# Values of the gated attention projected for two head pairs at once with tokens on partitions, sent to batch order through HBM, in a one-core early-fusion kernel

## The reference, cut to what matters

```python
# x (16,3,96,96), x_txt (16,32): 36 patch tokens + 32 text tokens = 68 per batch, 16 batches, 1088 tokens
h = concat(patch_embed(x), text_embed(x_txt))         # (16, 68, 256)
n = layernorm(h)
q, k, v = n @ W_q, n @ W_k, n @ W_v                   # 16 heads of 64
a = sigmoid(n @ W_gate + b_gate)                      # (16, 68, 16, 64)
# for each batch and head, over the 68 tokens:
#   S = a_t[:, None] * S + k_t[:, None] * v_t[None, :];   o_t = q_t @ S
h = h + out @ W_o
h = h + moe(layernorm(h))                             # 8 experts, top 2 of them, 256 -> 512 -> 256
```

## Time and profile before

| | |
|---|---|
| median of 3 runs | 406.86 us (405.18 to 407.86) |
| the profiled execution | 408.7 us; span of its trace 407.0 us |
| mean granted PE clock | 0.934 of full speed |
| busy: PE, PEld, DVE, ACT, POOL | 344.7, 299.4, 222.7, 132.4, 131.1 us |
| attention (first projection to last mix) | 38.1 to 221.2 us |
| steady pair step | 22.6 to 22.8 us |

### The profile page before, as it was taken

How to read it: one execution, slowest core, us unless ns; L and a number is a source line. 1 busy time by engine, 2 the same in 40 slices (tenths; PEclk the granted TensorE clock), 3 DMA queues, 4 the chain that set the end, 5 groups by cost and what they waited for, 6 DMA issues and landing times.

```text
span 407.0 us, 7752 instructions
## 1 busy us (share of the span) xinstructions
PE 344.7 (85%) x2739; PEld 299.4 (74%) x2740; DVE 222.7 (55%) x329; ACT 132.4 (33%) x279; POOL 131.1 (32%) x124
## 2 busy tenths in 40 slices
PE   4883997989989898989998999883499999999900
PEld 3663987888888888888987887573378888888800
DVE  0048799468484948577582145458235545544325
ACT  1143661444536253444344011431023223323300
POOL 5120043221312212222013699103506555554310
PEclk9997998999999999999999999966589999999965
DMA  7810011010010710000001930003102221122155
GB/s 208 289 52 2 0 53 52 4 52 2 2 53 0 317 45 0 0 0 0 1 1 26 439 159 0 0 2 110 52 26 68 66 77 65 70 70 66 41 165 202
DMA packets 10791, 28.85 MB, mean 71 GB/s; under 512 B 2000, under 2 KB 6608, under 8 KB 10128
## 3 DMA queue, kind: packets, MB, share of 16 engines
q1 hardware_dynamic: 8336, 21.99, 14.9%
q0 software_dynamic: 2432, 6.56, 5.6%
HBM read 23.17 MB, written 5.37 MB: 70 GB/s over the span
## 4 chain that ended last, share of the span: by engine, by line
PE 64%; DVE 9%; issue 9%; POOL 8%; DMA 7%; ACT 1%; SPq 1%; DVEq 0%; POOLq 0%; ACTq 0%
PE ps L716 10%; PE ps L381 8%; PE ps L503 7%; PE ps L382 7%; PE ps L383 7%; PE ps L518 5%; POOL w1lo L1415 5%; DVE U L1048 4%; PE ps L488 4%; PE ps L695 3%; PE ps L697 3%; PE ps L696 3%; PE ps L706 2%; POOL w1hi L1413 2%; DMA pt<-patches 2%
## 5 line engine op out<-in xcount | busy, mean ns | idle before, releaser
L381 PE MATMUL ps<-xnhi,wlo 128*128 128x272 f32 x256 | 77.4, 302 | 16.1 <-DVE kU L1054 9.0
L382 PE MATMUL ps<-xnlo,whi 128*128 128x272 f32 x256 | 75.5, 295 | 0.0
L383 PE MATMUL ps<-xnhi,whi 128*128 128x272 f32 x256 | 75.2, 294 | 0.0
L381 PEld LDWEIGHTS ps<-xnhi,wlo 128*128 128x128 f32 x256 | 49.9, 195 | 19.2 <-DVE kU L1054 10.4
L1062 DVE RECIPROCAL invU<-U 128x272 f32<-128x272 f32 x32 | 56.7, 1813 | 0.0
L943 ACT ACTIVATE hr<-ps,b 128x128 f32<-128x128 f32 x96 | 27.4, 367 | 81.3 <-PE ps L706 81.3
L1367 POOL TENSOR_TENSOR qA<-qraw,invU 128x544 f32<-128x544 f32 x16 | 22.3, 1392 | 95.3 <-DVE invU L1062 75.5
L382 PEld LDWEIGHTS ps<-xnlo,whi 128*128 128x128 f32 x256 | 49.8, 195 | 0.0
L383 PEld LDWEIGHTS ps<-xnhi,whi 128*128 128x128 f32 x256 | 49.7, 194 | 0.0
L1048 DVE TENSOR_TENSOR_SCAN U<-u_g,first 128x544 f32<-128x544 f32 x16 | 29.8, 1865 | 28.9 <-ACT u_g L827 28.9
L716 PE MATMUL ps<-w,hr 128*128 x192 | 45.2, 379 | 0.0
(11 more groups left out here) (166 smaller groups left out, 526.3 us busy)
## 6 DMA issues: line engine op xcount, KB each, us to landing
wraw<-w_attn SPq DMA_DIRECT2D x8, 512.5 KB, 3.4
w<-w SPq DMA_DIRECT2D x1, 4096.0 KB, 15.2
w<-w SPq DMA_DIRECT2D x1, 3072.0 KB, 10.6
yin<-yrows SPq DMA_DIRECT2D x4, 384.0 KB, 4.5
wo<-w_o SPq DMA_DIRECT2D x1, 1024.0 KB, 14.0
w<-w SPq DMA_DIRECT2D x1, 1024.0 KB, 5.9
b<-b SPq DMA_DIRECT2D x1, 1024.0 KB, 17.1
xrows<-xrow SPq DMA_DIRECT2D x2, 512.0 KB, 3.0
```

The costliest lines, as they stand in the source:

```text
L381: pe.matmul(dst, slo, mhi[n], start=(i == 0), stop=False)
L382: pe.matmul(dst, shi, mlo[n], start=False, stop=False)
L383: last = pe.matmul(dst, shi, mhi[n], start=False, stop=(i == len(pairs) - 1))
```

## The change

The values are no longer projected pair by pair. For two pairs at a time (`k`, 256 value columns) the roles are exchanged: 128 tokens of the activations are the stationary operand, 256 columns of the value weights move, and the result has tokens on partitions. Nine token tiles (the last of 64 tokens) make five chunks `j` per two pairs: four of 12 matmuls with 256 columns and one of six. ACT copies each chunk from bank 6 to one of two `vst` buffers, SP stores it to the HBM array `vrows` (256 KB a chunk, the last 64 KB), and `load_values(hp)` brings one pair back as 68 tokens on partitions, 16 batches of 128 columns: 557 KB in pieces of 512 bytes. So `vT`, the transposes (L488) and two ACT copies (L841, L847) go. The chunks are placed between the other work of earlier steps (`EVEN`, `ODD`, `FIRST`). Scores take the heads alternately. Queries, scores and mixes are interleaved; the last group of pair `hp-2` is mixed after the first gate of step `hp`; DVE takes scan, mask, scan, keys, keys. The gate's exponential goes straight to `u_g`. Steps 6 and 7 are written out without chunks. SP loads w1 one expert per step instead of six at once.

```diff
-MATS = 4
+MATS = 3
@@ sync
+            def store_values(k, j):
+                sp.wait_ge(s_vev, VC * k + j + 1)
...
+                    sp.dma_start(vrows[k, at:at + 2 * P].rearrange("(q p) d -> p q d", p=P), vst[j % 2][:]
+                                 ).then_inc(s_vst[j % 2], 16)
...
+            def load_values(hp):
+                for i in range(2):
+                    sp.wait_ge(s_vst[i], stored(hp // 2 + 1, i))
                 if hp >= 2:
+                    sp.wait_ge(s_omm, 4 * (hp - 1))
+                c = (hp % 2) * P
+                sp.dma_start(vb[hp % 2][0:T], vrows[hp // 2, :, c:c + P].rearrange("(b t) d -> t b d", t=T)
+                             ).then_inc(s_vb[hp % 2], 16)
...
+            load_value_weights(1)
+            for j in range(VC):
+                store_values(0, j)
+            load_values(0)
+            load_values(1)
+            for hp in range(1, HP):
+                if hp + 1 < HP:
+                    sp.wait_ge(s_wlo, hp)
+                    sp.dma_start(wraw[(hp + 1) % 2][:], w_attn[hp + 1, :, 0:WA + 1]).then_inc(s_wload[(hp + 1) % 2], 16)
+                k = hp // 2 + 1
+                if k < IT:
+                    for j in (range(VC) if hp == 1 else range(3) if hp % 2 == 0 else range(3, VC)):
+                        store_values(k, j)
+                if hp % 2 and k + 1 < IT:
+                    load_value_weights(k + 1)
+                if hp >= 2:
+                    load_values(hp)
+                if hp <= EARLY_W:
+                    sp.dma_start(w1[:, hp - 1], w_1[:, hp - 1]).then_inc(s_w1, 16)
@@ tensor, pair_step (before: projections, then turn_values / pair_scores / mix for each group)
+                project(hp, par, GATE, 0)
+                if not early(hp, 2):
+                    mix(hp - 2, par, G - 1, loaded[par])
+                pe.wait_ge(s_qraw, 2 * hp)
+                project(hp, par, GATE, 1)
...
+                pair_scores(hp - 1, 1 - par, 0)
+                pe.wait_ge(s_exp, 2 * hp + 1)
+                project(hp, par, KEY, 0)
+                chunk(1)
+                pe.wait_ge(s_exp, 2 * hp + 2)
+                project(hp, par, KEY, 1)
+                mix(hp - 1, 1 - par, 0, loaded[1 - par])
+                chunk(2)
+                pair_scores(hp - 1, 1 - par, 1)
+                pe.wait_ge(s_ku, 2 * hp + 1)
+                project(hp, par, QUERY, 0)
+                chunk(3)
+                mix(hp - 1, 1 - par, 1, loaded[1 - par])
+                pair_scores(hp - 1, 1 - par, 2)
+                chunk(4)
+                pe.wait_ge(s_ku, 2 * hp + 2)
+                project(hp, par, QUERY, 1)
+                mix(hp - 1, 1 - par, 2, loaded[1 - par])
+                pair_scores(hp - 1, 1 - par, 3)
+                chunk(5)
@@ scalar, pair_step
                 evacuate_gate(hp, par, 0)
+                if not early(hp, 2):
+                    evacuate_o(hp - 2, G - 1)
                 evacuate_gate(hp, par, 1)
                 if not tail:
                     split_pair(hp + 1, 1 - par, wload)
+                chunk(1)
+                evacuate_o(hp - 1, 0)
+                chunk(2)
                 evacuate_q(hp, 0)
+                chunk(3)
+                evacuate_o(hp - 1, 1)
+                chunk(4)
                 evacuate_q(hp, 1)
+                evacuate_o(hp - 1, 2)
+                chunk(5)
...
+            with act.Fori(1, IT - 1) as it:
+                split_values(it + 1)
+                pair_step(2 * it, 0, it + 1, EVEN, 16 * it + 16)
+                pair_step(2 * it + 1, 1, it + 1, ODD, 16 * it + 32)
```

More of the change, by code:

```diff
@@ L56 @@
 LN_EPS = 1e-5
-MATS = 4
-GATE, KEY, QUERY, VALUE = range(MATS)
+MATS = 3
+GATE, KEY, QUERY = range(MATS)
 WA = MATS * DC * P
+WG = WA + 1 + DC * P
+VW = 2 * P
+WV = DC * VW
+VT = -(-TOK // P)
+VC = -(-VT // 2)
+VTAIL = TOK - (VT - 1) * P
+IT = HP // 2
 WF = DC * FH
@@ L449, in first_projections @@
                 pe.wait_ge(s_std, 2)
-                project(0, 0, VALUE, 0)
+                pe.wait_ge(s_wvlo, 1)
+                first_values(0)
+                first_values(1)
                 pe.wait_ge(s_xnlo, 2)
-                for mat, read in ((GATE, s_exp), (KEY, s_ku), (QUERY, s_qraw), (VALUE, s_vt)):
+                for mat, read in ((GATE, s_exp), (KEY, s_ku), (QUERY, s_qraw)):
                     pe.wait_ge(read, 1)
                     project(0, 0, mat, 1)
[L456 to L485, removed]
+                    first_values(2 + mat)
+            def first_values(j):
+                if j >= 2:
+                    pe.wait_ge(s_vev, j - 1)
+                value_tiles(j, 4 + j % 2)
+            def value_tiles(j, bank):
+                for q in range(2 if j < VC - 1 else 1):
+                    r = 2 * j + q
+                    w = P if r < VT - 1 else VTAIL
+                    tok = slice(r * P, r * P + w)
+                    dst = ps[0:w, bank, q * VW:(q + 1) * VW]
+                    for m in range(DC):
+                        pe.matmul(dst, xnlo[:, m, tok], wvhi[:, m, :], start=(m == 0), stop=False)
+                        pe.matmul(dst, xnhi[:, m, tok], wvlo[:, m, :], start=False, stop=False)
+                        last = pe.matmul(dst, xnhi[:, m, tok], wvhi[:, m, :], start=False, stop=(m == DC - 1))
+                last.then_inc(s_vmm, 1)
@@ L486, in turn_values @@
                 for b in range(GB):
                     t = slice((GB * g + b) * T, (GB * g + b + 1) * T)
[L488 to L502, removed]
+                    for h in range(2):
+                        rows = slice(DK * h, DK * (h + 1))
@@ L521, in mix, with pair_step, chunk @@
                 last.then_inc(s_omm, 1)
[L523 to L530, removed]
+            def pair_step(hp, par, k, chunks, loaded):
+                def chunk(at):
+                    if at in chunks:
+                        values(k, chunks[at])
+                pe.wait_ge(s_wlo, hp + 1)
+                if early(hp, 2):
+                    pe.wait_ge(s_exp, 2)
+                    pe.wait_ge(s_ku, 2)
+                pe.wait_ge(s_qraw, 2 * hp - 1)
+                project(hp, par, GATE, 0)
[3 more added lines that the diff above has]
+                project(hp, par, GATE, 1)
+                if early(hp, 2):
+                    pe.wait_ge(s_vev, VC)
+                pair_scores(hp - 1, 1 - par, 0)
[18 more added lines that the diff above has]
+                chunk(5)
             embed_patches(0)
@@ L813, in split_pair, with split_values @@
                 act.activation(bneg[par][:], wraw[par][:, WA:WA + 1], ACT.Copy, scale=-1.0).then_inc(s_whi, 1)
+            def split_values(k):
+                act.wait_ge(s_wv, 16 * k + 16)
+                if not early(k, 1):
+                    act.wait_ge(s_vmm, VC * k)
+                act.activation(wvhi[:], wv[:], ACT.Copy).then_inc(s_wvhi, 1)
             def evacuate_gate(hp, par, c):
@@ L835, in evacuate_q, with evacuate_values @@
                 act.activation(half(qraw, c), slot(proj_slot(hp, QUERY, c)), ACT.Copy).then_inc(s_qraw, 1)
[L837 to L847, removed]
+            def evacuate_values(k, j, bank=6):
+                act.wait_ge(s_vmm, VC * k + j + 1)
+                act.wait_ge(s_vst[j % 2], stored(k, j))
+                if j < VC - 1:
+                    act.activation(vst[j % 2][:].rearrange("p q d -> p (q d)"), ps[:, bank, :], ACT.Copy
+                                   ).then_inc(s_vev, 1)
+                else:
+                    act.activation(vst[j % 2][0:VTAIL, 0], ps[0:VTAIL, bank, 0:VW], ACT.Copy).then_inc(s_vev, 1)
             def evacuate_o(a, g, bank=7):
@@ L877, in _ @@
             split_pair(0, 0, 16)
+            split_values(0)
             square(0)
@@ L1091, in _ @@
             dve.wait_ge(s_first, 1)
-            decay(0, 0)
+            for c in range(2):
+                scan(0, c)
+                decay_keys(0, 0, c)
+            in_bounds(0)
             for g in range(G):
```

199 lines of the change are left out of this document (118 added, 81 removed).

## The result

The changed kernel takes 430.63 us (median of 4 runs, 427.55 to 432.12), the kernel before 406.02 in the same runs: a ratio of 1.060 with an interval of 1.052 to 1.068. I forecast 415. The direction was right, and 430.6 lies inside the range; the size was not right: 24.6 us between the medians where the sum had 8.1. The profiled execution of after has a span of 425.8 us against 407.0, 18.8 more. It is the fastest of its four, the others had spans of 428.5 to 430.4 at mean clocks of 0.878 to 0.885 (0.887 in the profiled one), and that of before (408.7) lay 2.7 above the 406.02. So some 6 of the 24.6 us lie in executions of which no trace is shown here; what follows explains the 18.8.

A forecast was written before the change was run, and what follows sets the result against it. Attention was taken as bound by PE before the change, and by the value loads on four engines after; summed steps end attention at 229.3 against 221.2, +8.1, giving 416.8 profiled and 415 forecast, range 382 to 432.

The forecast's parts named there:

- The mechanism: Load of 68 partitions runs on 4 engines and holds mix 0; four engines at 26 to 40 ns: 0.60, 405 to 428.
- `wraw` behind two loads: Step 1: `wraw` for pair 2 queues behind loads 0 and 1, lands at 78.8; PE's second chunk waits until 80.5.
- The rival of the hidden load: Load on 16 engines takes 4.1 us, mix 0 never waits, kernel 382 us; hidden or nearly: chance 0.20.
- its clash: A step's second scan would start before POOL makes `wlo`, so 1.4 us of overlap with POOL go.
- step 2 was held by `wv`: In step 2 ACT waits for `wv`, holding the gate by 2.6 us and the step by 2.2, to 20.5.
- the load time of 10.6 us: Load of one pair's values on 4 engines: 272 x 0.032 + 1.9 = 10.6 us; mix 0 starts at 12.2.
- its term of 1.9 us: Fixed part of a load's time beside its pieces, 1.9 us, taken from 2.0 for a 64 KB transfer.
- The pieces: A load's 512-byte pieces at 32 ns each, bounds 20 and 51, 272 on each of 4 engines.
- the slow restart: After a pause PE runs 12 matmuls 0.24 us apart instead of 0.125, costing 1.4 us in steps 1 and 3 to 5.
- "No further loss": Steady steps: `wraw` lands at about 15, `evacuate_o(0)` ends by 16.5 as PE reaches mix 1, so nothing more is lost.
- "One microsecond of load time moves this by about 6": Kernel time per microsecond of load time: two in step 1, one in each of steps 3 to 6.
- The anchor: Profiled execution would be 416.8 us; before's profile lay 1.8 above its median, so the forecast was 415.

The follow-up runs named there:

- 2, 4 and 16 engines: The changed kernel with each load of values in two parts of 34 partitions (468.09 us, one execution), uncut (430.63 us), or in parts of 64 and 4 (390.9 us).
- the weights were early: Changed kernel, load in 64 and 4 partitions, `wv` issued before the stores, `wraw` a step earlier, POOL's `wvlo(1)` ahead of `qA` of pair 0: 380.0 us.

## Why the prediction was right or wrong

*The mechanism* was right and is shown: four engines (2, 4 and 16 engines give 468, 431 and 391 us), mix 0 of steps 3 to 6 held by the load, step 1 by `wraw` behind two loads. The rival of the hidden load lost; it had 382 us, and with 16 engines the kernel came to 391, and to 380 once the weights were early. I had also forecast a wait for the load at mix 0 of step 1, and the changed kernel has none there (mix 0 starts at 70.48).

*Step by step,* predicted and measured, from one first gate to the next:

| | 1 | 2 | 3 | 4 | 5 | 6 | 7 | last pair |
|---|---|---|---|---|---|---|---|---|
| predicted | 37.6 | 20.5 | 22.6 | 24.8 | 22.6 | 19.7 | 20.0 | 6.0 |
| measured | 37.2 | 21.0 | 26.9 | 27.55 | 24.6 | 22.0 | 18.65 | 6.7 |

The first gate of step 1 lies at 55.8 (55.5), that of step 2 at 93.0 (93.1), and the reason holds: `wraw` behind two loads lets ACT start at 77.94 (78.8), and the second chunk starts at 79.50 (80.5). One wait there I had not seen: `wvlo(1)` stands behind `qA` of pair 0 on POOL, and PE's first chunk waits for it for 3.9 us. It cost nothing, because the second chunk was held until 79.50 in any case. Scores take 0.64 (0.65), the second scan lost its clash (mean 1313 ns for 1865), step 2 was held by `wv` as said. Step 7 is 1.35 better than forecast.

*The step that failed is the load time of 10.6 us in steps 3 to 6, in its term of 1.9 us for all that is not pieces.* From issue to mix 0 the four loads took 13.5, 12.2, 11.9 and 11.6 us. The pieces were priced right or a bit dear (8.7 us; 7.8 measured). The fixed part came from a 64 KB transfer of another shape; beside the pieces 3.8 to 5.7 us passed. About 2.5 of them are the load's own, as pair 0 shows. The rest I had put at nothing: the forecast lets `w1` and `wraw` come after the load and gives them no effect on it, nor does it give any to the store ahead. Which of them made the loads late is open. Mix 0 started 15.0, 14.25, 13.4 and 13.0 us after the first gate where I had 12.2: 6.9 us in four steps.

*The second term too small is the slow restart,* 1.4 us each from 12 slow matmuls. Behind mix 0 of step 3 the slow stretch goes from 128.98 to near 135. Counted against full speed, the mix and the score lose 0.49 and 0.46, twelve matmuls of the query 1.25 and five of the values 0.5: 2.7 us. From mix 0 to the next gate the four steps took 4.5 us more than forecast in all. Together 11.4 us; with +0.5 in step 2 and +0.7 at the end, less 1.35 in step 7 and 0.1 at the start of step 2, that is the 11 between 229.3 and 240.4.

*"No further loss" behind mix 0 was true only by a hair.* I had `wraw` landing at 15 and so harmless. It lands at 17.1 after the first gate, because SP could not issue it for 7 us. The loss was hidden behind the load's own, and would have stood alone without it: the run with mix 0's batches first gained 4 us, that with `wraw` and `wv` early, POOL's order changed and `w1` late 10, both together 36. "One microsecond of load time moves this by about 6" is therefore not a slope that goes far below the measured load time: `wraw` takes over some 3.5 us down (mix 1 of step 3 starts at 135.99 in the changed kernel and at 132.50 with mix 0 free).

*The anchor.* I took 1.8 us off because the profile of before lay above its median; that of after lay 3.1 below its own. Those 4.9 us of the miss of 15.6 are not explained by any trace.

## What to carry to other kernels

Before a transfer's bytes are priced, look at how its partitions divide: 68 put half a megabyte on 4 engines, and 64 + 4 took 40 us off the kernel without another byte moved. When a long transfer is found to hold an engine, look for what was issued behind it and who waits for that on an in-order engine: there were two holders here in parallel, and the removal of either one alone was worth a fraction of both. Split a load by who needs it first, price what it takes beside its bytes by a transfer of the same form and with the same neighbours in the queue, and try parts of a change alone: one line of it (heads in turn) made the kernel before 2% faster while the whole made it 6% slower.

## What the runs showed of the hardware

A DMA issued right behind a single 68-partition load of 1088 pieces held SP for 5.6 to 8.3 us, while one behind the 64 + 4 form took 0.35 (`w1`) and 0.42 us (`wraw`). A piece of 512 bytes cost 28.8 ns on 4 engines (71 GB/s, 17.8 each; 33 ns in one load at 62 GB/s) and 25.6 on 2 (40 GB/s, 20 each). Scores of 16 matmuls with 64 rows take 0.64 us when the two halves of the rows alternate and 0.94 in blocks. After pauses of 7.0, 5.3, 5.4 and 5.0 us in steps 3 to 6 a mix took 1.17 or 1.18 us in place of 0.69: the granted clock had fallen to 0.50, that is 1.2 GHz, during the pause. In step 3 the slow stretch lasted from 128.98 to near 135, and then TensorE ran at 2.4 GHz again.
